# A state-space and mixture-of-experts layer: another order of the same steps on each engine

## The reference

```python
# LayerNorm, then h = LN(x) * (1 + ca) + sa, x: (8, 2048, 256)
zxbcdt = h @ W_in
xBC = silu(causal_dwconv(xBC, conv_w, conv_b))          # 4 taps
dt = softplus(dt + dt_bias); A = -exp(A_log)
y = _ssd(x, dt, A, Bm, Cm) + x * D                      # chunked state-space scan, 8 heads of 64
y = y * silu(z); y = y * rsqrt(mean(y * y) + EPS) * norm_w
x = x + ga * (y @ W_out)
# LayerNorm again, h = LN(x) * (1 + cb) + sb
gate_logits = softmax(h @ gate_w + gate_b)              # 8 experts
weights = gate_logits * (gate_logits >= 0.1), divided by their sum
for e in range(8): out = out + weights[:, e:e+1] * (h @ expert_w[e] + expert_b[e])
x = x + gb * out
```

## Time and profile before

| | us |
|---|---|
| median of 3 runs (2538.1 to 2542.51) | 2540.7 |
| the profiled execution | 2534.47 |
| its span, first to last instruction | 2532.8 |
| TensorE busy | 2340.5 |
| VectorE busy | 2120.1 |
| ScalarE busy | 1434.0 |
| GpSimd busy | 1272.9 |

### The profile page before, as it was taken

How to read it: one execution, slowest core, us unless ns; L and a number is a source line. 1 busy time by engine, 2 the same in 40 slices (tenths; PEclk the granted TensorE clock), 3 DMA queues, 4 the chain that set the end, 5 groups by cost and what they waited for, 6 DMA issues and landing times.

```text
span 2532.8 us, 48158 instructions
## 1 busy us (share of the span) xinstructions
PE 2340.5 (92%) x14936; PEld 1952.9 (77%) x14936; DVE 2120.1 (84%) x4582; ACT 1434.0 (57%) x3788; POOL 1272.9 (50%) x1428
## 2 busy tenths in 40 slices
PE   2689999999999999999999999999999999999998
PEld 2578788877787778788787787887788787878876
DVE  4478888888889888888878888988888988888876
ACT  1376655565555655665555655556655556566551
POOL 1155545545545545545545544555545554554553
PEclk6699999999999999999989999999999999999999
DMA  3000000000000000000000000000000000000000
...
DMA packets 62922, 59.08 MB, mean 23 GB/s; under 512 B 10096, under 2 KB 62160, under 8 KB 62672
## 3 DMA queue, kind: packets, MB, share of 16 engines
...
...
## 4 chain that ended last, share of the span: by engine, by line
issue 55%; POOL 22%; PE 11%; DVE 9%; ACT 2%; POOLq 1%; DMA 0%; SPq 0%; DVEq 0%; ACTq 0%
POOL y L394 4%; PE pe L1122 4%; POOL state L389 4%; POOL xs L375 3%; PE pa L1122 3%; POOL x L405 3%; POOL xd L381 2%; POOL x L434 2%; DVE y L898 2%; PE pd L1122 2%; DVE feat L810 1%; DVE eacc L999 1%; DVE e3in L865 1%; POOL eacc L430 1%; PE py L1122 1%
## 5 line engine op out<-in xcount | busy, mean ns | idle before, releaser
L999 DVE SCALAR_TENSOR_TENSOR eacc<-pe,wg,eacc 128x256 f32<-128x256 f32 x1024 | 491.6, 480 | 53.9 <-PE pe L1122 24.2
L1122 PE MATMUL pe<-e_hi,h_hi 128*128 128x512 f32 x1024 | 467.2, 456 | 19.1 <-DVE eacc L999 16.9
L810 DVE SCALAR_TENSOR_TENSOR feat<-pa,cw,feat 128x512 f32<-128x512 f32 x576 | 429.0, 745 | 39.5 <-ACT feat L521 30.9
L583 ACT ACTIVATE lm<-pd,e3in 128x128 f32<-128x128 f32 x1024 | 289.0, 380 | 247.6 <-PE pd L1122 247.6
L1122 PE MATMUL pe<-e_lo,h_hi 128*128 128x512 f32 x1024 | 410.1, 400 | 0.0
L1122 PE MATMUL pe<-e_hi,h_lo 128*128 128x512 f32 x1024 | 407.2, 398 | 0.0
L594 ACT ACTIVATE lm<-lm,lndt 128x128 f32<-128x128 f32 x1024 | 328.0, 407 | 0.0
L521 ACT ACTIVATE feat<-pa,cb,cw 128x512 f32<-128x512 f32 x192 | 149.2, 777 | 264.8 <-PE pa L1122 264.8
L1122 PEld LDWEIGHTS py<-xt,mm 128*128 128x128 f32 x2048 | 242.6, 193 | 40.8 <-DVE mm L880 25.9
L1122 PE MATMUL pa<-h_hi,w_hi 128*128 128x260 f32 x768 | 231.7, 302 | 44.2 <-DVE feat L810 40.1
L394 POOL TENSOR_TENSOR y<-y,xd 128x512 f32<-128x512 f32 x128 | 164.4, 1285 | 211.4 <-DVE y L888 211.2
...
## 6 DMA issues: line engine op xcount, KB each, us to landing
xin<-_attn_hidden_states_dram SPq DMA_DIRECT2D x32, 512.0 KB, 4.1
xres<-_attn_hidden_states_dram SPq DMA_DIRECT2D x128, 128.0 KB, 2.1
out_dram<-x SPq DMA_DIRECT2D x128, 128.0 KB, 2.1
...
mm<-in_L_attn_W_out_dram SPq DMA_DIRECT2D x1, 512.0 KB, 7.1
```

Source lines behind the costliest of these rows:

```text
L583: last = act.activation(lm[:, h], pd[:, h // 4, h % 4 * P:(h % 4 + 1) * P], ACT.Relu, scale=-1.0, bias=e3in[:, x.q, 0, x.t, h:h + 1])
L810: dve.scalar_tensor_tensor(out=acc, in0=pa[:, :, 1 + j:1 + j + HT], scalar=cw[:, f, j:j + 1], in1=acc, op0=ALU.mult, op1=ALU.add).then_inc ...
L999: dve.scalar_tensor_tensor(out=eacc[:, x.j], in0=pe_[:, i % 2, e * DM:(e + 1) * DM], scalar=wg[:, x.q, x.t, c:c + 1], in1=eacc[:, x.j], op ...
L1122: return pe.matmul(o, lhsT=l, rhs=r, start=start, stop=stop, skip_group_check=True)
```

## The change

The bodies of the five loops are put in another order; the steps, their waits, their instructions, the tensors and the buffers stay. All steps are still in every loop once as often as before (9 on SP, 43 on GpSimd, 61 on ScalarE, 109 on VectorE, 72 on TensorE). Some steps cross the loop's end: `M_(4)` at the end of VectorE's list is now `M_(8)` at its start, which is the same place, `D_(3)` at the end of TensorE's is now `D_(7)` at its start, behind `e1`, `e2`, `state_` and `ydiag_`; `e2` of TensorE and `xD0`, `xD1` of VectorE for the tile n - 14, which stood at the start of a pass, are now in the pass before, as n - 10. The diff of SP's and GpSimd's lists, and of the parts of the others around the steps spoken of below:

```diff
                 sp.dma_start(out_tok[x.n * P:(x.n + 1) * P], x2[:, x.n % NX2]).then_inc(s_out[x.n % NX2], 16)
 
             for n in range(-4, NTILE + 16, T):
+                do(load_xres, sp, n - 6)
+                do(store, sp, n - 14)
                 do(load_xres, sp, n - 5)
+                do(store, sp, n - 13)
+                do(store, sp, n - 12)
                 do(load_xin, sp, n + 4)
-                do(store, sp, n - 15)
                 do(load_xres, sp, n - 4)
+                do(store, sp, n - 11)
                 do(load_xres, sp, n - 3)
-                do(store, sp, n - 14)
-                do(store, sp, n - 13)
-                do(load_xres, sp, n - 2)
-                do(store, sp, n - 12)
 
             for i, o in enumerate(s_out):
                 sp.wait_ge(o, 16 * len(range(i, NTILE, NX2)))
...
                 pool.tensor_tensor(x2[:, x.n % NX2], eacc[:, x.j], x2[:, x.n % NX2], ALU.add).then_inc(S["out"], 1)
 
             for n in range(-4, NTILE + 16, T):
-                do(x2r_, pool, n - 9)
+                do(h2lo_, pool, n - 12)
                 do(out_, pool, n - 15)
                 do(ve2_, pool, n - 10)
                 do(rstd2_, pool, n - 10)
+                do(scd_, pool, n - 7)
                 do(xd_, pool, n - 7)
                 do(xs_, pool, n - 7)
                 do(rs_, pool, n - 8)
-                do(scd_, pool, n - 7)
-                do(n_ve, pool, n)
-                do(h2lo_, pool, n - 10)
                 do(y2_, pool, n - 7)
                 do(og_, pool, n - 14)
+                do(out_, pool, n - 14)
+                do(x2r_, pool, n - 8)
                 do(scd_, pool, n - 6)
-                do(out_, pool, n - 14)
                 do(xd_, pool, n - 6)
+                do(og_, pool, n - 13)
+                do(rs_, pool, n - 7)
+                do(out_, pool, n - 13)
                 do(xs_, pool, n - 6)
+                do(x2r_, pool, n - 7)
+                do(y2_, pool, n - 6)
+                do(h2lo_, pool, n - 10)
+                do(n_ve, pool, n)
                 do(n_rstd, pool, n)
-                do(rs_, pool, n - 7)
-                do(y2_, pool, n - 6)
-                do(og_, pool, n - 13)
-                do(x2r_, pool, n - 8)
-                do(x2r_, pool, n - 7)
+                do(scd_, pool, n - 5)
                 do(xd_, pool, n - 5)
                 do(ve2_, pool, n - 8)
+                do(rstd2_, pool, n - 8)
                 do(xs_, pool, n - 5)
-                do(rstd2_, pool, n - 8)
                 do(y2_, pool, n - 5)
                 do(n_lo, pool, n)
-                do(scd_, pool, n - 5)
-                do(out_, pool, n - 13)
-                do(n_lo, pool, n + 2)
                 do(rs_, pool, n - 6)
                 do(og_, pool, n - 12)
+                do(n_lo, pool, n + 2)
                 do(out_, pool, n - 12)
-                do(h2lo_, pool, n - 8)
+                do(x2r_, pool, n - 6)
+                do(xs_, pool, n - 4)
                 do(xd_, pool, n - 4)
+                do(og_, pool, n - 11)
+                do(scd_, pool, n - 4)
                 do(halo, pool, n + 4)
-                do(scd_, pool, n - 4)
-                do(xs_, pool, n - 4)
-                do(og_, pool, n - 11)
-                do(x2r_, pool, n - 6)
                 do(rs_, pool, n - 5)
+                do(x2r_, pool, n - 5)
                 do(y2_, pool, n - 4)
 
         @block.scalar
```

VectorE, around the gate and behind the taps, and at the end:

```diff
-                do(n_ag, dve, n + 2)
-                do(xn2_, dve, n - 10)
                 do(yTlo_, dve, n - 8)
                 do(xn2_, dve, n - 9)
+                do(xD0, dve, n - 13)
+                do(xD1, dve, n - 13)
                 do(tA3, dve, n - 4)
+                do(n_ag, dve, n + 1)
                 do(tB3, dve, n - 4)
-                do(xD0, dve, n - 13)
                 do(tC3, dve, n - 4)
                 do(M_, dve, n - 7)
                 do(n_st, dve, n + 3)
-                do(xD1, dve, n - 13)
+                do(S_, dve, n - 7)
+                do(xD2, dve, n - 13)
+                do(n_ag, dve, n + 2)
                 do(x2_, dve, n - 8)
-                do(S_, dve, n - 7)
+                do(tA4, dve, n - 4)
                 do(lg_, dve, n - 10)
-                do(n_ag, dve, n + 3)
-                do(h2hi_, dve, n - 10)
+                do(tB4, dve, n - 4)
                 do(lgx_, dve, n - 12)
-                do(tA4, dve, n - 4)
-                do(tB4, dve, n - 4)
-                do(xD2, dve, n - 13)
                 do(tC4, dve, n - 4)
                 do(y3_, dve, n - 7)
+                do(gate_, dve, n - 12)
                 do(y4_, dve, n - 7)
-                do(gate_, dve, n - 12)
+                do(wg3_, dve, n - 12)
+                do(xD3, dve, n - 13)
                 do(tA5, dve, n - 4)
                 do(tB5, dve, n - 4)
+                do(n_ag, dve, n + 3)
                 do(tC5, dve, n - 4)
-                do(xD3, dve, n - 13)
-                do(n_xn, dve, n)
-                do(n_xn, dve, n + 1)
...
+                do(xD1, dve, n - 11)
                 do(parts_, dve, n - 4)
+                do(n_hi, dve, n + 2)
+                do(lg_, dve, n - 8)
+                do(x2_, dve, n - 6)
+                do(y3_, dve, n - 5)
                 do(h2hi_, dve, n - 8)
-                do(S_, dve, n - 5)
-                do(n_hi, dve, n + 2)
-                do(y3_, dve, n - 5)
-                do(x2_, dve, n - 6)
-                do(lg_, dve, n - 8)
-                do(xD0, dve, n - 11)
+                do(xD2, dve, n - 11)
+                do(es_, dve, n - 4)
                 do(y4_, dve, n - 5)
-                do(es_, dve, n - 4)
-                do(xD1, dve, n - 11)
-                do(xD2, dve, n - 11)
+                do(xD3, dve, n - 11)
+                do(gs_, dve, n - 4)
+                do(n_st, dve, n + 4)
+                do(xD0, dve, n - 10)
+                do(yTlo_, dve, n - 5)
                 do(tA0, dve, n)
                 do(tB0, dve, n)
                 do(tC0, dve, n)
-                do(gs_, dve, n - 4)
-                do(xD3, dve, n - 11)
-                do(n_st, dve, n + 4)
-                do(yTlo_, dve, n - 5)
+                do(xD1, dve, n - 10)
+                do(st2_, dve, n - 6)
                 do(y1_, dve, n - 4)
```

More of the change, by code:

```diff
@@ L1069, in _ @@
+                do(dtb, dve, n - 2)
+                do(st2_, dve, n - 8)
+                do(n_xn, dve, n + 1)
                 do(S_, dve, n - 6)
                 do(xD0, dve, n - 12)
-                do(st2_, dve, n - 8)
+                do(ag2_, dve, n - 8)
                 do(st2_, dve, n - 7)
+                do(ag2_, dve, n - 7)
+                do(y3_, dve, n - 6)
+                do(y4_, dve, n - 6)
+                do(dtb, dve, n - 1)
                 do(xD1, dve, n - 12)
+                do(xD2, dve, n - 12)
@@ L1074, in _ @@
+                do(nabs_, dve, n - 4)
+                do(xn2_, dve, n - 8)
                 do(n_xn, dve, n + 2)
-                do(dtb, dve, n - 2)
-                do(y3_, dve, n - 6)
-                do(ag2_, dve, n - 8)
-                do(y4_, dve, n - 6)
-                do(xD2, dve, n - 12)
-                do(ag2_, dve, n - 7)
-                do(dtb, dve, n - 1)
-                do(y1_, dve, n - 5)
-                do(nabs_, dve, n - 4)
-                do(w1_, dve, n - 4)
-                do(xn2_, dve, n - 8)
@@ L1331, in _ @@
             for n in range(0, NTILE + 16, T):
+                do(D_, pe, n - 7)
+                do(e3_, pe, n - 14)
                 do(ft2, pe, n - 4)
                 do(xT_, pe, n - 7)
-                do(e2, pe, n - 14)
+                do(e0, pe, n - 13)
+                do(bias_, pe, n - 13)
                 do(G_, pe, n - 7)
@@ L1359, in _ @@
+                do(wgT_, pe, n - 12)
                 do(z_, pe, n - 4)
+                do(bias_, pe, n - 12)
                 do(wout_, pe, n - 7)
-                do(wgT_, pe, n - 12)
+                do(e1, pe, n - 12)
                 do(z_, pe, n - 3)
-                do(bias_, pe, n - 12)
+                do(state_, pe, n - 6)
                 do(D_, pe, n - 5)
-                do(state_, pe, n - 6)
-                do(e1, pe, n - 12)
                 do(z_, pe, n - 2)
+                do(ydiag_, pe, n - 6)
```

125 lines of the change are left out of this document (61 added, 64 removed).

## The result

The changed kernel takes 2390.25 us (median of 4 runs, 2387.1 to 2397.88), the kernel before beside it 2539.4 us (4 runs, 2535.17 to 2542.51): a ratio of 0.942 (95% interval 0.9392 to 0.9445). The forecast was 2426 us. The profiled execution of the changed kernel took 2397.88 us with a span of 2396.2.

What follows compares the result with a forecast made beforehand. TensorE's waits on VectorE and GpSimd, about 5.5 us of a 74.4 us group, were the winnable part. Period 74.4 - 0.8 - 0.9 - 0.7 - 0.5 + 0.4 - 0.6 = 71.3, giving 2426 us; range 2385 to 2505.

Steps and rivals of the forecast that it cites:

- case A: The forecast case, chance 0.56: plain period 70 to 72.5 us, whole time 2390 to 2458 us.
- (a): GpSimd: rs_(6) in front of n_lo(2) ends the chain making TensorE wait at D_(4); gain 0.8 us a group.
- (b): VectorE: xD1(11) right behind M_(5), y4_(5) and es_ later, so e3_(11) stops waiting; gain 0.9 us a group.
- (c): TensorE: more work ahead of ydiag_(5) removes its wait for M_(5); gain 0.72 us, csT_ perhaps 0 to 0.4 late.
- (d): Taps and gating: waits at ft5, z_(4), wout_(7), 1.7 us, become one of about 1.2 at z_(4); gain 0.5.
- L959 still long: Sign that the forecast is right: VectorE's lgt instruction stays lengthened, meeting GpSimd's scd_(6) again (1.05 us).
- (e): Stretch after z_: n_xn(0) waits for n_rstd behind h2lo_(10), making TensorE wait at xT_(5); cost 0.4 us, 0 to 1.5.
- (f): SP: load_xin behind two stores has about 1 us to spare before n_st(4); cost nothing, up to 0.5 us.
- (g): Groups with gt_: xD3(13) is ready, so no wait; 0.6 us over a plain group instead of 4.2.
- B: Rival, chance 0.20: GpSimd still lengthens VectorE's instructions as now, 3.0 us instead of 1.0; period 73.8, time 2501 us.
- C: Rival, chance 0.12: tC5 comes late and z_(4) waits 2.8 us instead of 0.4; period 76.6, time 2575 us.
- D: Rival, chance 0.08: waits at z_(4) drop TensorE's clock in every group; period 75.5, 2541 us, no change.

Runs made afterwards that it cites:

- e2: Kernel before with only rs_(6) moved in front of n_lo(2) on GpSimd: 2485.64 us, ratio 0.9817, plain period 72.65 us.
- e12: Kernel before with only xD1(11) moved in front of y4_(5) and es_ on VectorE: 2523.91 us, ratio 0.9961.
- e3: Kernel before with three moves: gt_ behind z_(4), rs_(6) ahead of n_lo(2), xD1(11) ahead of y4_(5) and es_: 2508.48 us, ratio 0.9917.
- e11: Changed kernel with rs_(6) put back behind n_lo(2) on GpSimd: 2410.98 us, ratio to the kernel before 0.9512.
- e5: Changed kernel with n_ve and n_rstd moved in front of h2lo_(10) on GpSimd: 2383.36 us, ratio to the kernel before 0.9405.
- e4: Changed kernel with one added GpSimd instruction of about 1.04 us per group beside VectorE's gating: 2422.89 us, ratio to the kernel before 0.9577.
- e9: The changed kernel run again without edits: 2393.07 us (5 runs), ratio to the kernel before 0.9441.
- e8: Changed kernel with an added GpSimd instruction of about 1.04 us per group beside VectorE's last taps: 2413.23 us, ratio to the kernel before 0.9519.

## Why the prediction came out as it did

The direction, the places of the waits and the size of most terms held; the time came out 36 us below the forecast, at the lower end of case A (2390 to 2458) and 5 us inside the stated range. Where these are: 27 x (71.3 - 70.35) = 25.7 us in the plain period, less 7 in the groups above plain (11.5 us in all, forecast 4.2), 2.7 in fill and drain: 21 us of span (2417 and 2396.2). The other 15 come from going from the profiled execution to the median: I added 6.2 us, since before was that much above its profile, and rounded 1 us up, but this time the profiled execution was the longest of four and 7.6 above the median. That is scatter between executions, and a forecast should have put it in the range, not in the sum.

**(a) and (b), right in sum, wrong in their split.** Forecast 0.8 + 0.9 = 1.7; e2 shows 1.75 from (a) alone in the old order. That the sum is right is luck: one wait was priced at half of its worth, and the other half given to a move that did not earn it. The wait of xD1(11) and y4_'s 1.81 us were both the late x2_(6), 1.36 us earlier. The step of (b) that failed is the sentence that its 0.92 us go because xD1 is moved: alone that move is worth 0.35 (e12), and together with (a) it loses 0.95 (e3). In the new order y4_(5), two instructions further on, takes 0.68 us; there (a) is worth some 0.3 us of the period (e11).

**(c), right; a term too high.** The wait at ydiag_(5) is gone. I charged M_(5) 1.9 us because it "still starts beside n_lo(0)". It does, but 0.03 us ahead of it, in each of the 27 passes, and the other engine pays:

```profile
1011.60 1.22 DVE L880 TENSOR_TENSOR mm<-lm,gs 128x1024 f32<-128x1024 f32 x1
```
```profile
1011.63 2.32 POOL L355 TENSOR_TENSOR h_lo<-hf,h_hi 128x512 fp32r<-128x512 f32 x1 [3.64 <-DVE h_hi L796]
```

In the kernel before it was the other way round:

```profile
1062.07 1.87 DVE L880 TENSOR_TENSOR mm<-lm,gs 128x1024 f32<-128x1024 f32 x1 [0.16 <-ACT lm L594]
```
```profile
1061.58 1.28 POOL L355 TENSOR_TENSOR h_lo<-hf,h_hi 128x512 fp32r<-128x512 f32 x1 [3.99 <-DVE h_hi L796]
```

csT_ doesn't wait either (forecast 0.2).

**(d), the term that was mis-sized.** Forecast: 1.2 us at z_(4), out of 1.0 us of lengthening in the gating. Measured from ft2 (1035.26) to z_(4) (1059.04): 23.78 us, and 23.41 without the wait, which start to start is 0.37 (0.73 from `wgT_` to z_(4), and 0.36 in the passes in which z_(4) has no wait). TensorE's own 23.4 was exact. The start of ft2, and VectorE's tC5:

```profile
1035.26 0.28 PE L1122 MATMUL pa<-h_hi,w_hi 128*128 128x260 f32 x1
```
```profile
1058.23 0.75 DVE L810 SCALAR_TENSOR_TENSOR feat<-pa,cw,feat 128x512 f32<-128x512 f32 x1
```

VectorE ended tC5 at 1058.98, 23.72 after ft2, where I had 23.3 to 23.7 without any lengthening and a microsecond more with it. `lgt` was to meet scd_(6); it met only its end:

```profile
1051.75 0.28 DVE L959 TENSOR_TENSOR lgt<-lgt,gmax 128x32 f32<-128x32 f32 x1
...
1053.86 0.19 DVE L969 SCALAR_TENSOR_TENSOR wsel<-pr 128x32 f32<-128x32 f32 x1
```
```profile
1050.94 1.04 POOL L389 TENSOR_TENSOR state<-state,e 128x512 f32<-128x512 f32 x1
```

0.28 us instead of 1.28, because scd_ ends at 1051.98. "L959 still long" was wrong (median 281 ns, has 1278), "L969 near 191" right (192). The 0.83 us at z_(4) and csT_'s 0.2 are 1.03, a little more than 71.3 - 70.35 = 0.95.

**(e), right.** Forecast 0.4 at xT_(5); from ydiag_ to xT_ it is 2.17 us (1068.04 to 1070.21) and 1.76 in e5, so 0.41. VectorE's two waits there, 2.35 us for dtb(3) and 2.65 for n_xn(0), were forecast as 2.3 and 2.9.

**(f), right.** Behind the fill VectorE waits for `xin` three times, 0.4 to 0.6 us each (near 740, 880 and 1447 us), about the 0 to 0.5 of the forecast; these passes are as long as others of their kind (70.34, 72.46 and 70.90 us).

**(g), right for the group, wrong for the sum.** A group with `gt_` takes 0.53 us over a plain one (70.88 and 70.35, forecast 0.6), and `gt_` has no wait and no half clock behind it:

```profile
1480.88 0.69 PE L1122 MATMUL pe<-grow,ident 8*128 8x512 f32 x1
```

But five passes have a stretch at half clock, and that I had given no term. Three are plain ones, 1.3 us each (71.65 against 70.35), and two have `gt_`, 1.6 each (72.46 against 70.88); there the stretch stands ahead of `gt_`. Together it is some 7 of the 11.5 us that the passes have above 27 plain ones.

**The rivals.** B (turns not taken) fell (its sum has a slip, 27 x 73.8 + 4.2 is 1997 and not 2001, which would put it at 2497 us): what is still lengthened on VectorE in the plain group is small (L860 0.74 us instead of 0.19, L898 once 0.93 instead of 0.69, L946 once 0.63 instead of 0.42), and its busy time is 5.6 us less. C was right in its kind and wrong in its price. tC4 had 1.1 us of lead, under the 1.5 from which C was to decide, but from tC4's end (1052.69) to tC5's (1058.98) VectorE needed 6.3 us and not 7.6, since the gating with its small instructions unheld was short; e4, which holds one of them, has the wait of 1.4 us that this would give. D is there in part: half clock in 5 of 27 passes (7 in e9, 17 in e8) at one place of the pass, some 55 us behind its start. Not by the mechanism of D, though. Behind z_(4)'s and xT_(5)'s waits the clock stays at 1.00, and it does so in e4 too, where z_(4) in the plain passes without a fall waits 1.4 us, longer than the 1.2 of which D spoke. In the ten microseconds ahead of each of the five falls TensorE's record has no gap; the rows below show the last two. The DMA burst beside a fall stands also in passes without one.

```profile
906.00:908.00 2.00, 2.00 (x20) 2.00 (x20) 1.97 (x6) 0.78 (x1) 0.57 (x1) 1.00 0.00 0
908.00:910.00 2.00, 2.00 (x16) 1.73 (x16) 1.97 (x7) 0.77 (x4) 1.15 (x2) 0.78 0.42 117
910.00:912.00 2.00, 2.00 (x6) 1.41 (x6) 1.76 (x10) 1.52 (x6) 0.00 (x0) 0.50 0.04 14
...
1052.00:1054.00 2.00, 2.00 (x12) 1.68 (x13) 1.90 (x7) 1.94 (x9) 0.00 (x0) 1.00 0.39 130
```

What makes it fall in one pass and not in the next stays open: no run here changed it alone.
